# TensorE's arms of an expert take the next expert's first twelve matmuls along, and the program ends without GpSimd's drain

## The reference

```
x = x + rwkv_attention(layernorm(x))      # first phase
x = x + moe(layernorm(x))                 # second phase
# moe, per sequence of 1024 tokens: top 2 of 8 experts, at most 320 tokens to an expert
h   = silu(tokens @ w1[e]) * (tokens @ w3[e])    # 256 -> 896
out = (h @ w2[e]) * weight                       # 896 -> 256, added to the token's row
```

## Time and profile before

| what | value |
|---|---|
| time, median of 3 runs | 855.15 us (853.99 to 855.53) |
| the profiled execution's own time | 854.25 us |
| its span in the trace | 852.2 us |
| phase B on TensorE | from about 349 us |
| expert 1, 3, 5 (with a rest) | 70.9, 70.9, 71.0 us |
| expert 2, 4, 6 (without) | 61.1, 61.2, 60.8 us |
| TensorE busy share, granted clock | 95%, 0.99 |

### The profile page before, as it was taken

The page is one execution under the profiler, slowest core; times in us unless marked ns, Lnnn a source line. Parts: engine busy times, 40 slices in busy tenths (PEclk is TensorE's granted clock), DMA queues, the critical chain, the costliest instruction groups (busy, mean ns, idle before and its releaser), DMA issues. The chain is left out here.

```text
span 852.2 us, 17481 instructions
## 1 busy us (share of the span) xinstructions
PE 812.1 (95%) x6343; PEld 677.2 (79%) x6343; DVE 499.1 (59%) x1237; ACT 490.7 (58%) x876; POOL 462.0 (54%) x497
## 2 busy tenths in 40 slices
PE   3999999999999998999999999999999999999995
PEld 2678887777788776787997788997788898888884
DVE  6888888899888767343542443543543544443441
ACT  4578888888888787354643543643543543552431
POOL 6454476777787756475434355434356443436214
PEclk9999999999999999999999999999999999999998
DMA  5852132113111122654334145333334342404113
GB/s 149 342 196 70 34 117 74 52 52 96 42 50 65 53 78 75 208 157 82 101 67 91 59 106 94 100 68 40 109 95 72 92 110 28 121 2 51 20 14 42
DMA packets 50474, 74.05 MB, mean 87 GB/s; under 512 B 5056, under 2 KB 42176, under 8 KB 50368
## 3 DMA queue, kind: packets, MB, share of 16 engines
q1 hardware_dynamic: 35488, 53.46, 19.1%
q0 software_dynamic: 14592, 19.18, 13.5%
q10 hardware_dynamic: 288, 0.01, 0.0%
HBM read 38.41 MB, written 34.22 MB: 85 GB/s over the span
## 5 line engine op out<-in xcount | busy, mean ns | idle before, releaser
L1592 POOL DMA_INDIRECT out<-ysb,index x80 | 124.7, 1559 | 145.3 <-DVE ysb L1831 111.5
L1945 PE MATMUL p<-xh,whi 128*128 128x512 f32 (+2 forms) x504 | 185.6, 368 | 6.1 <-issue 5.2
L1807 DVE TENSOR_TENSOR hid<-gated,p 128x512 f32<-128x512 f32 (+1 forms) x126 | 81.1, 643 | 181.1 <-ACT gated L1654 181.1
L1947 PE MATMUL p<-xh,wlo 128*128 128x512 f32 (+2 forms) x504 | 185.3, 368 | 0.0
L1946 PE MATMUL p<-xl,whi 128*128 128x512 f32 (+2 forms) x504 | 184.6, 366 | 0.0
L1971 PE MATMUL py<-w,hh 128*128 128x512 f32 x448 | 162.6, 403 | 3.7 <-DVE hl L1088 3.0
L1654 ACT ACTIVATE gated<-p 128x512 f32<-128x512 f32 (+1 forms) x126 | 71.0, 564 | 162.2 <-PE p L1947 162.2
L1581 POOL TENSOR_TENSOR wlo<-wraw,whi 128x448 fp32r<-128x448 f32 x56 | 70.7, 1266 | 94.7 <-ACT whi L1640 90.6
L1945 PEld LDWEIGHTS p<-xh,whi 128*128 128x128 f32 x504 | 94.7, 188 | 23.4 <-issue 8.0
L1970 PE MATMUL py<-w,hl 128*128 128x256 f32 x384 | 108.6, 283 | 0.0
L1946 PEld LDWEIGHTS p<-xl,whi 128*128 128x128 f32 x504 | 94.8, 188 | 15.3
(11 more groups left out here) (204 smaller groups left out, 1440.4 us busy)
## 6 DMA issues: line engine op xcount, KB each, us to landing
wraw<-in_w SPq DMA_DIRECT2D x24, 896.0 KB, 4.8
disp<-wraw SPq DMA_DIRECT2D x16, 662.5 KB, 9.3
xtok<-disp SPq DMA_DIRECT2D x16, 530.0 KB, 4.9
x_ring<-in_x SPq DMA_DIRECT2D x16, 256.0 KB, 3.5
out<-x SPq DMA_DIRECT2D x16, 256.0 KB, 2.2
xtok<-disp SPq DMA_DIRECT2D x8, 265.0 KB, 4.2
out<-ysb,index POOLq DMA_INDIRECT x80, 3.8
disp<-row,slot_i POOLq DMA_INDIRECT x64
```

The lines of the kernel that those rows point to most:

```text
L1592: nc.gpsimd.indirect_dma_start(out, bass.IndirectOffsetOnAxis(ap=index[e.const % 2][:, t:t + 1], axis=0), ysb[j % NY][:], None, compute_op ...
L1807: nc.vector.tensor_tensor(hid[k][:, 0:w], gated[k][:, 0:w], p3[k][:, 0:w], ALU.mult).then_inc(hid_ready, 1)
L1945: nc.tensor.matmul(dst[:, 0:w], hi[m][:, wcut], xh[xcut], start=(kt == 0), stop=False)
L1947: ins = nc.tensor.matmul(dst[:, 0:w], lo[m][:, wcut], xh[xcut], start=False, stop=(kt == KT - 1))
```

## The change

Four edits, all on TensorE's program but the last:

1. `up` gets an argument `slices`, and a new function `begin(e)` does the first slice (f = 0, twelve matmuls) of `up(e, 1)` for experts 1 to 6. Every arm of `step` ends with `begin(e + 1)`, ahead of the join; `step` itself begins with slices 1 to 6. No matmul is added or dropped.
2. `first` no longer uses `with_rest_where_taken` and joins late: both arms hold everything to the end of expert 0, including `last_chunk` and `begin(1)`.
3. Expert 0's Else arm no longer loads the count a second time and waits for nothing with `pass_over` at its end: its last down adds the two skipped tiles' counts with its own increment (`skipped`).
4. The block is opened with `no_gpsimd_drain=True`.

```
+BEGUN = range(1)
...
-            with nc.Block() as block:
+            with nc.Block(no_gpsimd_drain=True) as block:
...
-        def up(e, c, tiles=None):
+        def up(e, c, tiles=None, slices=range(FT)):
...
-            for f in range(FT):
+            for f in slices:
...
-                down(e, t, moved if t == MOVED else None, skipped if t == MOVED else 0)
+                down(e, t, moved if t == MOVED else None, skipped if t == sum(CHUNKS[2]) - 1 else 0)
...
-            with_rest_where_taken(e, lambda: down(e, t0 + n - 1))
-            last_chunk(e)
-            down_rest(e, COMMON)
+            i = e.count()
+            n_taken = pe.value_load(taken[0:1, i:i + 1])
+            with pe.If(n_taken > COMMON * P):
+                turn(e, TB - 1)
+                down(e, t0 + n - 1)
+                up(e, 0)
+                last_chunk(e)
+                down_rest(e, COMMON)
+                begin(e + 1)
+            with pe.Else():
+                pass_over(pe, e, (turned, TB - 1, TB, 1))
+                down(e, t0 + n - 1)
+                pass_over(pe, e, (h_done, chunk_at(e, 0) * FT, HPE, FT))
+                last_chunk(e, None, REST)
+                begin(e + 1)
+
+        def begin(e):
+            if e.const < E - 1:
+                up(e, 1, slices=BEGUN)
 
         def step(e):
-            up(e, 1)
+            up(e, 1, slices=range(BEGUN.stop, FT))
...
                 for t in range(COMMON, sum(tiles)):
                     down(e, t, (0, MOVED), ST - sum(tiles) if t == sum(tiles) - 1 else 0)
+                begin(e + 1)
...
                 last_chunk(e, None, REST)
+                begin(e + 1)
```

More of the change, by code:

```diff
@@ L1996, in rest_where_taken @@
             where_taken(pe, e, COMMON, up_rest, lambda: pass_over(pe, e, (turned, TB - 1, TB, 1), (h_done, n, HPE, FT)))
[L1998 to L2011, removed]
         def last_chunk(e, moved=None, skipped=0):
```

## The result

The changed kernel takes **843.1 us** (median of 4 runs, 842.06 to 843.76); the kernel before, on the same chip, 854.57 us (853.52 to 855.53). The ratio is 0.9863, 95% interval 0.9846 to 0.988: 11.5 us less. The profiled execution took 843.76 us with a span of 841.8 us; it was the slowest of its four.

A forecast was written before the change was run, and what follows sets the result against it. TensorE, busy 95% of the span, was taken as the bound. 854.25 - 4.60 (drain) - 4.14 (three joins) - 0.35 (expert 0) = 845.16 us, by the median 846.06; stated 845.6, range 843.4 to 850.7.

The forecast's parts named there:

- What bounds the kernel, and what "issue" is: TensorE, busy 95%, bounds it; its 5.2 us of "issue" waits are sequencer jumps at the joins behind experts 1, 3, 5.
- The drain, 4.60 us: At the block's end GpSimd's DRAIN stands alone for 4.605 us; opening the block without it saves 4.60 us.
- The rival in which it comes back: The drain's work returns outside the span, which grows what lies around it by up to 4.6 us; 849.8 us, chance 0.18.
- The cover, 3.50 us: At joins behind experts 1, 3, 5, queued matmuls, twelve now wide, keep TensorE busy 3.50 us during the jump, against 2.12 before.
- The rival of a much deeper queue: At the joins, a deeper lead (documented depth 64) or 3.3 us jumps hide the whole jump; 843.6 us, chance 0.07.
- the mean of the three jumps, 3.84: Jump length at joins behind experts 1, 3, 5, taken as unchanged at 3.84 us.
- The loss forecast: Each join behind experts 1, 3, 5 still loses 0.51 us instead of 1.89, saving 4.14 us for three.
- Expert 0, 0.35 us: Expert 0's join saves 0.46 us; its Else jump, now taken as far (3.7 us), costs 0.1; net 0.35 us.
- The Else jumps of experts 2, 4, 6: Jumps to the Else arms at L2047 stay as they are; no gain and no cost.
- Landing in cold code: Rival: after far jumps at three joins and expert 0's arm, a second fetch costs up to 15 us; 860.4 us, chance 0.04.
- whole jump hidden: Case in which the three joins lose nothing, saving 5.67 us; time 843.6 us, chance 0.07.

The follow-up runs named there:

- e1: The kernel before with only the block opened with no_gpsimd_drain=True, TensorE's program untouched; 850.35 us, ratio 0.9941 to the kernel before.
- e4: The changed kernel with only six of the twelve matmuls begun in the arms, six behind the join; 846.87 us, ratio 0.9894 to the kernel before.
- e10: The changed kernel with two slices (24 matmuls) begun in the arms; 854.63 us, ratio 0.9931, the kernel before taking 862.33 us in that group.
- e11: The changed kernel with two slices begun, count loaded between slices 4 and 5, 64 never-run instructions added to move landings; 849.04 us, ratio 0.9855 to the kernel before.
- e7: The kernel before without the 80 indirect DMAs adding the expert results to token rows, semaphores incremented by GpSimd instead; 850.3 us, one execution.
- e12: Second run of e7's kernel (the kernel before without the results' 80 indirect DMAs); 855.5 us, one execution, the kernel before taking 862.3.
- e2: The changed kernel with GpSimd's drain kept (plain nc.Block()); 847.91 us, ratio 0.9901 to the kernel before.
- e3: The changed kernel with expert 0 as before (small arms, second load and branch, waiting pass_over, begun matmuls behind its join); 848.42 us, ratio 0.991 to the kernel before.
- e5: e3 with 38 instructions more in expert 0's If arm, which never runs; 844.94 us, ratio 0.9887 to the kernel before.
- e6: The changed kernel with 79 instructions more in expert 0's If arm, which never runs; 847.13 us, ratio 0.991 to the kernel before.
- e8: The changed kernel with the count loaded ahead of the remaining up matmuls instead of behind them; 843.39 us, ratio 0.9867 to the kernel before.
- e9: The changed kernel run again, unaltered, in a later group; 849.90 us, ratio 0.9871, the kernel before taking 862.33 us there.

## Why the prediction missed, step by step

- **What bounds the kernel, and what "issue" is:** right. TensorE's few waits and the end were all that moved.
- **The drain, 4.60 us:** right. The end is 4.7 us shorter in the trace, 5.0 (3.3 to 6.8) by e1. The rival in which it comes back is excluded: 1.9 us lie around the span, 2.05 before.
- **The cover, 3.50 us:** right, 3.47 wherever one slice is begun and the jump is long enough to tell. e4 confirms the formula at 2.8 us, and e10 and e11 at two slices. The rival of a much deeper queue falls.
- **The jump, "the mean of the three jumps, 3.84": this is the term that failed.** In the changed kernel's profile the three took 3.50, 3.24 and 3.31 us, 3.35 on average. The loss forecast was 0.51 us a join; it was 0.07 on average, so the joins gave 5.5 us where 4.14 stood. I took 3.84 us as a property of the join because the three values agreed so well. The twelve matmuls also shift the jump against GpSimd's DMAs: the last one had been issued 1.8 us ahead of it, now it is 0.3 us. That this shift shortened the jumps is argued from e7 and e12 and not shown: e4 on one side and e10 and e11 on the other have a DMA issued at nearly the same moment, 0.4 us into the jump, and their jumps took 3.40 and 3.75 us on average. With one slice begun, 21 jumps in seven runs (after, e2, e3, e5, e6, e8, e9) took 3.24 to 4.18 us, 3.60 on average, with the packet starting late (1.3 us or more) in only 5 of 21, against five of six with the program of before. By the mean the saving is 1.6 us a join; the changed kernel's profile, at 3.35, was on the lucky side of that. The Else jumps, 3.30 to 3.80 in the trace of before, had shown such a spread; I used them as a bound and not for the value.
- **Expert 0, 0.35 us:** right in mechanism. The jump was far (3.85 us for 480 instructions, where I had counted 526 without the sequencer's own), the late down used up the 0.67 us wait for hl and cost nothing at all, and the join gave 0.49 us, where 0.46 less 0.1 had been reckoned.
- **The Else jumps of experts 2, 4, 6:** no net change; two of them gave 0.48 us together, the third took 0.51.
- **"Landing in cold code", 0.04:** it did not happen in this kernel, but it is real, and it was rated far too low. Four of the kernels run here (e3, e4, e6, e10) have it; it costs 0.6 to 2.4 us a place by starts. The changed kernel's six landings missed the bad stretch by luck: nothing in its design put them there. The argument against it, that none of the old landings showed it, said nothing about new positions.
- **The rest:** the medians moved 11.5 us, the two profiles 10.4. The profiled execution of the changed kernel was the slowest of four and its first phase 0.6 us late. The range's low end had been set at the "whole jump hidden" case, 843.6, with no room for the spread of runs (1.7 us in the four); that alone would have held 843.1.

Not settled: why a jump varies from 3.29 to 3.79 us even at the joins of e7 and e12, where no DMA packet but the instruction queue's starts ahead of the jump's end, and what GpSimd's drain waits for.

## What to carry to other kernels

A far jump of a sequencer could be hidden here, and no edit to TensorE's program was shown to shorten it: put the widest instructions at hand, independent of the arm, ahead of it, and reckon cover = what the queue holds x their distance against a jump whose length has a spread, not a value. Keep register loads and waits away from both the jump and the landing. And in a program with far jumps any edit moves all later landings against the instruction blocks; before an edit is blamed or praised for a microsecond, look for idle places inside a run of plain matmuls, a fixed count behind a landing, and shift them with instructions in code that isn't run.

## What the hardware showed unexpectedly

- TensorE's sequencer was 17 or 18 matmuls with their loads ahead, not more, whatever their width: from the jump's start they lasted 2.11 us where all were narrow, 2.79 with six wide (e4), 3.47 with twelve wide, and 3.94 to 4.16 us of wide alone (e8, e10).
- Each far jump of experts 1 to 6 has a 16 KB packet on the instruction queue, begun 0.9 to 1.9 us into it (the 4.18 us jump of e5 has one more, at 0.07 us), and was over 2.3 to 2.9 us after that packet's start. The jumps lay in 3.24 to 4.2 us; other branches took 0.07 us (not taken) and 0.2 to 0.4 (short ones).
- Where TensorE had to wait for the next block, it followed 3.0 to 4.0 us behind a landing at the joins and 4.4 to 4.6 at the Else landings.
- GpSimd's drain at the end took 4.605 us in two kernels (before, e2) and 5.304 us in both runs of a third (e7, e12), to the nanosecond; at the start of the program it took 0.174.
